# Batch 0's row maxima from float32 scores in four row groups, in a one-core attention and MLP layer

## The reference

```python
q1, q2 = split_heads(x @ Wq1, 16), split_heads(x @ Wq2, 16)      # 16 features a head
k, v = split_heads(x @ Wk, 16), split_heads(x @ Wv, 16)
q = concatenate([q1, q2], axis=1)                                # 32 query heads
scores = einsum('bhqd,bhkd->bhqk', q, repeat(k, 2)) * 0.25       # pairs of query heads share k, v
p = softmax(where(causal, scores, min))
y = p @ repeat(v, 2)
y = y[:, :16] - sigmoid(x @ Wlam) * y[:, 16:]
x = layernorm(x + y @ Wo)
out = layernorm(x + shared_mlp(x) + routed_mlp(x) * comb_w)
```

## Time and profile before

| | |
|---|---|
| median of 3 runs | 467.77 us (466.49 to 467.85) |
| profiled execution, its own time | 466.94 us |
| its span in the profile | 465.2 us |
| busy: PE, VectorE, ScalarE, POOL | 417.3, 282.7, 234.9, 244.6 us |
| granted TensorE clock, mean | 0.958 |
| moved by DMA | 40.41 MB |

### The profile page before, as it was taken

How to read it: one execution, slowest core, us unless ns; L and a number is a source line. 1 busy time by engine, 2 the same in 40 slices (tenths; PEclk the granted TensorE clock), 3 DMA queues, 4 the chain that set the end, 5 groups by cost and what they waited for, 6 DMA issues and landing times.

```text
span 465.2 us, 10336 instructions
## 1 busy us (share of the span) xinstructions
PE 417.3 (90%) x4008; PEld 339.7 (73%) x4008; DVE 282.7 (61%) x676; ACT 234.9 (51%) x532; POOL 244.6 (53%) x334
## 2 busy tenths in 40 slices
PE   4229697899999999999999999999999999997995
PEld 4127246696799768994998669985898579856995
DVE  3637237753658557764758466755767478747474
ACT  4704481539334853567254944476355922592240
POOL 8314483629355754668254945576365922492152
PEclk9859798979999999999999999999999999999899
DMA  8762770346012810363123610381034410000000
GB/s 284 245 162 63 198 196 2 88 117 151 1 46 85 204 46 4 108 156 69 46 61 108 163 46 25 103 198 33 24 85 112 117 46 0 4 1 25 1 25 23
DMA packets 34753, 40.41 MB, mean 87 GB/s; under 512 B 4240, under 2 KB 28304, under 8 KB 34448
## 3 DMA queue, kind: packets, MB, share of 16 engines
q1 hardware_dynamic: 34704, 39.75, 31.6%
HBM read 27.94 MB, written 11.53 MB: 85 GB/s over the span
## 4 chain that ended last, share of the span: by engine, by line
PE 71%; POOL 9%; DVE 8%; ACT 4%; DMA 3%; issue 2%; SPq 2%; POOLq 0%; DVEq 0%; ACTq 0%
PE ff L672 11%; PE ff L673 10%; PE ff L674 10%; PE ring L735 7%; POOL prob L413 6%; PE ybank L787 5%; PE ybank L672 4%; PE ring L730 4%; PE ring L759 3%; PE ybank L673 3%; PE ybank L674 3%; PE ring L763 2%; ACT prob L518 2%; DVE neg_max L1020 2%; PE ybank L800 2%
## 5 line engine op out<-in xcount | busy, mean ns | idle before, releaser
L1020 DVE TENSOR_REDUCE neg_max<-ring 128x2 f32<-128x512 f32 (+3 forms) x176 | 102.7, 638 | 39.1 <-PE ring L735 38.5
L403 POOL TENSOR_TENSOR h_lo<-h_full,h_hi 128x256 fp32r<-128x256 f32 x72 | 52.9, 735 | 101.6 <-ACT h_hi L478 101.6
L413 POOL TENSOR_SCALAR_AFFINE_SELECT prob<-prob 128x512 f32<-128x512 f32 x128 | 82.9, 679 | 15.6 <-ACT prob L518 14.5
L672 PE MATMUL ff<-x1T_hi,wg_lo 128*128 128x256 f32 x288 | 87.2, 303 | 0.0
L518 ACT ACTIVATE prob<-ring 128x512 f32<-128x512 f32 x144 | 78.3, 620 | 6.9 <-PE ring L759 6.9
L673 PE MATMUL ff<-x1T_lo,wg_hi 128*128 128x256 f32 x288 | 81.2, 282 | 0.0
L674 PE MATMUL ff<-x1T_hi,wg_hi 128*128 128x256 f32 x288 | 81.0, 281 | 0.0
L730 PE MATMUL ring<-mask_b,ident_b 128*128 128x128 bf16 (+2 forms) x176 | 45.4, 258 | 18.9 <-DMA q_stack<-qk_parts_dram 17.1
L1041 DVE COPY yv<-ybank 128x256 f32<-128x256 f32 x64 | 27.0, 422 | 56.9 <-PE ybank L787 56.5
L735 PE MATMUL ring<-k_stack,q_stack 96*128 96x256 bf16 (+3 forms) x512 | 60.9, 239 | 0.0
L787 PE MATMUL ybank<-prob,v_ones 128*32 128x256 f32 (+1 forms) x1024 | 56.3, 335 | 2.0 <-POOL prob L413 1.8
(11 more groups left out here) (169 smaller groups left out, 962.7 us busy)
## 6 DMA issues: line engine op xcount, KB each, us to landing
q_stack<-qk_parts_dram SPq DMA_DIRECT2D x48, 256.0 KB, 4.5
qk_parts_dram<-parts SPq DMA_DIRECT2D x72, 128.0 KB
k_stack<-qk_parts_dram SPq DMA_DIRECT2D x48, 128.0 KB, 4.4
xt_raw<-xT SPq DMA_DIRECT2D x8, 256.0 KB, 2.8
xz<-x SPq DMA_DIRECT2D x8, 256.0 KB, 2.8
out<-xz SPq DMA_DIRECT2D x7, 256.0 KB, 2.2
prob<-w_gu SPq DMA_DIRECT2D x1, 1152.0 KB, 7.3
yv<-w_gu SPq DMA_DIRECT2D x1, 1024.0 KB, 9.1
```

Source lines behind the costliest of these rows:

```text
L403: pool.tensor_tensor(h_lo[:, n, :], h_full[:, n % RING, :], h_hi[:, n, :].bitcast(F32), ALU.subtract).then_inc(h_lo_done, 1)
L413: pool.affine_select(out=v, in_=v, compare_op=ALU.is_ge, fill=0.0, base=0, pattern=[[0, 2], [HALF, 2], [0, 2], [1, HALF]], channel_multipl ...
L672: pe.matmul(o, lhs_lo, rhs_hi, start=first, stop=False)
L1020: dve.tensor_reduce(neg_max[:, columns.start:columns.stop, i], ring[u % RING][:, 0:len(columns) * keys].rearrange("p (h k) -> p h k", k=keys),
```

## The change

**First scores.** In batch 0 the 22 units of `s_unit` are replaced by 24 units in six quads (`first_quad`). The queries are copied as float32 from PSUM (`first_query`), and the keys twice (`first_keys`), with a per-partition factor of 1 or 0 so that one copy holds the even heads' keys and one the odd heads' (`make_parity`). The copies lie in the second set of query stacks, unused until batch 1's loads. A head's product then has 32 rows, of which 16 are zero in the keys. The four units of a quad use the four row groups of the array and four banks (`ff` 0 and 1, `ring` 0, `misc`), and their head products are issued in turn. Each unit has a mask matmul as before. A unit of the next quad waits for the maximum of the unit four before. Quad 0 waits for the copies, the first parts and all three rests of batch 0. Behind quad 0 stand the two value jobs, behind quads 1, 2 and 3 the three projection jobs of batch 1. The wait for the stacks stands ahead of the transposed scores.

**Order of the start.** POOL makes the identity matrices first and the memsets of the k_stacks last. SP loads batch 1's x and the first gate/up piece ahead of batch 0's stores, and the other two pieces behind batch 0's twelve loads. Batch 1's parts are stored after `load_max(0)` and after the stacks of batch 0 have landed. ScalarE splits batch 1's x and the first gate/up piece behind batch 0's values, POOL subtracts both (in the kernel before VectorE subtracts all three pieces). The other two pieces are split on ScalarE behind `max_first(0)`, and subtracted on VectorE behind `max_second(0)`, as are w_out and the router.

```diff
+ROW_GROUP = 32
+FIRST_HEADS = HEADS * ROW_GROUP // P
+FIRST_TILE_HEADS = (4, 4, 2, 2)
+FIRST_JOBS = tuple((i, g * FIRST_HEADS + j * heads, heads) for i, heads in enumerate(FIRST_TILE_HEADS)
+                   for j in range(FIRST_HEADS // heads) for g in range(P // ROW_GROUP))
+FIRST_V_AT, FIRST_QK_AT = 0, (1, 2, 3)
...
             def iteration(i, has_next=True, has_last=True):
                 load_x(i)
-                if has_next:
+                if has_next and not is_first(i):
                     store_parts(i + 1, range(QK_JOBS))
                 if i + 2 < B:
                     load_xt(i + 2)
                 load_max(i)
+                if is_first(i):
+                    sp.wait_ge(stack_loaded, 16 * STACK_LOADS)
+                    store_parts(i + 1, range(QK_JOBS))
...
-            for n, (k, cols, raw) in enumerate(GU_PIECES):
-                sp.dma_start(raw, w_gu[k * P:(k + 1) * P, cols]).then_inc(wg_loaded[n], 16)
+            load_xt(1)
+            load_gate_up(0)
             for n, p in ((0, 0), (1, 0), (0, 1), (2, 0), (1, 1), (2, 1), (0, 2), (1, 2), (2, 2)):
                 store_part(0, n, p)
-            load_xt(1)
             load_stacks(0)
+            for n in range(1, len(GU_PIECES)):
+                load_gate_up(n)
...
+            k, cols, raw = GU_PIECES[0]
+            split_xt(1)
+            split_weight(1, wg_lo[:, k, cols], raw, wg_hi[:, k, cols], prob_raw_done)
...
                 split_weight(wp_hi[:, :, proj_chunk(c)], wp_raw[:, :, proj_chunk(c)], wp_loaded[c])
-                if c > 0:
-                    first_part(0, c - 1)
+            first_query(0)
+            first_part(0, 0)
             split_weight(wp_hi[:, :, proj_chunk(QK_JOBS)], wp_raw[:, :, proj_chunk(QK_JOBS)], wp_loaded[QK_JOBS])
-            second_part(0, 0)
+            first_query(1)
+            first_part(0, 1)
+            first_keys()
             first_part(0, QK_JOBS - 1)
-            for n in range(1, QK_JOBS):
+            for n in range(QK_JOBS):
                 second_part(0, n)
             act.wait_ge(consts_made, CONSTS)
             for t in range(TT):
                 values(0, t)
+            split_xt(1)
+            k, cols, raw = GU_PIECES[0]
+            split_weight(wg_hi[:, k, cols], raw, wg_loaded[0], mlp_w_hi_done)
...
+            def first_quad(n):
+                quad = range(QUAD * n, QUAD * (n + 1))
+                if n == 0:
+                    pe.wait_ge(q_first_done, Q_JOBS)
+                    pe.wait_ge(k_first_done, PARITIES)
+                    pe.wait_ge(qk_h_done, QK_JOBS)
+                    pe.wait_ge(qk_rest_done, QK_JOBS)
+                for u in quad:
+                    if n > 0:
+                        pe.wait_ge(max_done, u - QUAD + 1)
+                    i, first, heads = FIRST_JOBS[u]
+                    keys = (i + 1) * HALF
+                    o = first_bank(u)[:, 0:heads * keys].rearrange("p (h k) -> p h k", k=keys)
+                    pe.matmul(o[:, :, keys - HALF:keys], ident_b[:, :], mask_b[:, :].unsqueeze(1).to_broadcast([P, heads, HALF]),
+                              start=True, stop=False, skip_group_check=True)
+                i, _, heads = FIRST_JOBS[QUAD * n]
+                keys = (i + 1) * HALF
+                for j in range(heads):
+                    for u in quad:
+                        row, block = spot(FIRST_JOBS[u][1] + j)
+                        rows = slice(row // 2 * ROW_GROUP, (row // 2 + 1) * ROW_GROUP)
+                        mm = pe.matmul(first_bank(u)[:, j * keys:(j + 1) * keys], q_first[rows, block, i * P:(i + 1) * P],
+                                       k_first[rows, row % PARITIES, block, 0:keys], start=False, stop=True, skip_group_check=True)
+                        if j == heads - 1:
+                            mm.then_inc(s_full, 1)
...
+                for n in range(0 if has_prev else FIRST_QUADS):
+                    first_quad(n)
+                    if n == FIRST_V_AT:
...
+                        for t in range(TT):
+                            v_job(0, t)
+                    if n in FIRST_QK_AT:
+                        qk_job(1, FIRST_QK_AT.index(n))
+                for u in range(S_UNITS if has_prev else 0):
```

More of the change, by code:

```diff
@@ L49 @@
 CONSTS = 6
+PARITIES = 2
 ROUTER_STEPS = 5
@@ L148, in build_layer @@
         minus_half = sb("minus_half", [P, TT])
+        parity = sb("parity", [P, PARITIES])
         gate_t = sb("gate_t", [P, RING, T])
@@ L336, in _ @@
         def _(pool):
+            pool.memset(ident[:, :], 0.0).then_inc(const_step, 1)
+            pool.memset(ident_b[:, :], 0.0).then_inc(const_step, 1)
             pool.memset(xz[2][:, :, :], 0.0).then_inc(consts_made, 1)
             pool.wait_ge(consts_made, 1)
[L339 to L343, removed]
+            pool.wait_ge(const_step, 2)
+            for m in (ident, ident_b):
+                pool.affine_select(out=m[:, :], in_=m[:, :], compare_op=ALU.not_equal, fill=1.0, base=0,
+                                   pattern=[[-1, P]], channel_multiplier=1).then_inc(consts_made, 1)
             pool.memset(mask_b[:, :], 0.0).then_inc(const_step, 1)
@@ L346, in _ @@
             pool.memset(minus_half[:, :], -0.5).then_inc(const_step, 1)
[L347 to L350, removed]
+            pool.wait_ge(const_step, 5)
             for h in range(2):
@@ L358, in _ @@
             pool.memset(v_ones[:, :, :, HEAD_DIM:HEAD_DIM + 1], 1.0).then_inc(consts_made, 1)
+            pool.wait_ge(consts_made, CONSTS)
+            for k_stack in k_stacks:
+                pool.memset(k_stack[STACK_ROWS:STACK_ROWS + MAX_PARTS, :, :, :], 1.0).then_inc(const_step, 1)
+            pool.wait_ge(const_step, 5 + STACKS)
             def split_xt(b):
@@ L427, in iteration @@
             def iteration(i, has_next, has_prev, has_last):
-                if has_next:
+                if has_next and has_prev:
                     split_xt(i + 1)
@@ L482, in split_xt, with first_query, first_keys @@
                 copy(xt_hi[:, :, :], xt_raw[:, :, :]).then_inc(xt_hi_done, 1)
+            def first_query(n):
+                act.wait_ge(qk_full, n + 1)
+                copy(q_first[:, n, :].rearrange("p (i h t) -> p h i t", h=2, i=Q_TILES), psum_order(qk_bank(0, n)[:, :])).then_inc(q_first_done, 1)
+            def first_keys():
+                act.wait_ge(qk_full, QK_JOBS)
+                act.wait_ge(parity_made, PARITIES)
+                for x in range(PARITIES):
+                    act.activation(k_first[:, x, :, :], qk_bank(0, QK_JOBS - 1)[:, :].rearrange("p (n t) -> p n t", n=KEY_BLOCKS), ACT.Copy,
+                                   scale=parity[:, x:x + 1]).then_inc(k_first_done, 1)
             def raw_part(b, n):
@@ L933, in iteration @@
                     gu_units(i - 1, FF_MAX)
+                if not has_prev:
+                    pe.wait_ge(stack_loaded, 16 * STACK_LOADS)
                 pe.wait_ge(max_loaded, (i + 1) * (16 * MAX_PARTS))
@@ L1022, in row_max, with first_max, make_parity @@
                                   negate=True).then_inc(max_done, 1)
+            def first_max(u):
+                dve.wait_ge(s_full, u + 1)
+                i, first, heads = FIRST_JOBS[u]
+                keys = (i + 1) * HALF
+                dve.tensor_reduce(neg_max[:, first:first + heads, i], first_bank(u)[:, 0:heads * keys].rearrange("p (h k) -> p h k", k=keys),
+                                  AX_X, ALU.max,
+                                  negate=True).then_inc(max_done, 1)
+            def make_parity():
+                dve.wait_ge(consts_made, 2)
+                for x in range(PARITIES):
+                    dve.tensor_reduce(parity[:, x:x + 1], ident[:, :].rearrange("p (g x d) -> p x g d", x=PARITIES, d=HEAD_DIM)[:, x, :, :],
+                                      AXES_XY, ALU.add).then_inc(parity_made, 1)
             def max_second(b):
@@ L1167, in iteration @@
                 max_second(i)
+                if not has_prev:
+                    split_weight(W_OUT, wo_lo[:, :, :], wo_raw, wo_hi[:, :, :])
+                    split_weight(W_ROUTER, wr_lo[:, :, :], wr_raw, wr_hi[:, :, :])
+                    for n, (k, cols, raw) in enumerate(GU_PIECES[1:]):
+                        split_mlp_weight(n + 2, wg_lo[:, k, cols], raw, wg_hi[:, k, cols])
+                    dve.wait_ge(v_done, TT)
                 attn[0](dve.tensor_scalar(lam[:, :, :], lam_th[:, :, :], 0.5, 0.5, ALU.mult, ALU.add))
```

93 lines of the change are left out of this document (55 added, 38 removed).

## The result

The changed kernel takes 461.82 us as the median of 4 runs (459.52 to 462.41), the kernel before 467.81 beside it; the ratio is 0.9871, with a 95% interval of 0.9839 to 0.9903. The forecast was 461.0, in a range of 456.5 to 467.0. The profiled execution took 462.41 us, the longest of the four, with a span of 460.7.

A forecast was written before the change was run, and what follows sets the result against it. TensorE bounds the kernel, except early, where batch 0's maxima wait for stack loads until the first transposed score at 52.17. Profiled 466.94 less 6.2 is 460.7; the median was given as 461.0, range 456.5 to 467.0.

The forecast's parts named there:

- The first score: Batch 0's first transposed score matmul, after the maxima land: at 46.0 us against 52.17, 6.2 us less.
- Start of quad 0: First quad of batch 0, right behind VectorE's rest of the keys (job 2): starts at 16.6 us.
- Both of my readings of the row of L787: Float32 column groups, full clock: 49 ns per record or 2.06 ns per column; greater taken per head step, 0.40, 0.53 for 256 keys.
- rival 1: Quads' row groups overlap fully and clock stays up: maxima end at 39.3, scores start at 42.7, 457.5 us; chance 0.25.
- Clock: PE in the quads: quad 0 at 1.2 GHz, and 1.0 us added for quad 4 or 5 at half clock.
- ScalarE ahead of the maxima: Batch 1's split parts before the first maxima: POOL's gate/up piece 5.5 us, ScalarE free at 39.3, 3.6 us before needed, hidden.
- The rule on mode switches: Changing PE's tiling mode drains the engine: twice a quad, twelve times, at 0.2 each 2.4 us more, 463.4.
- the forecast's 0.2 for a handover: Estimated 0.2 us for the handover in each of quads 2 to 5, where PE and VectorE take turns.
- The down weights: End of batch 0: issued 57.6 to 58.8, last landed 65.9; ScalarE's wait hidden before y's split at 68.2, 0.8 us spare.
- the 22.2 that the prediction had named as a sign of being wrong: Batch 0's y split coming later than 22.2 us after the first transposed score would show the prediction wrong.
- Rival 3: Stores and loads take 3 to 4 us longer, so ScalarE is some 3 late for y and value copies: 464.0; chance 0.15.
- the 0.3 us that I added: Final step: 461.0 given, between 460.7 for the profiled execution and a median of runs 0.8 above that execution.

The follow-up runs named there:

- dup_max: Changed kernel with the last eight maxima reductions (quads 4 and 5) each made twice on VectorE; 468.73 us, ratio 1.001 to the kernel before.
- down_early: Changed kernel with the three down-weight loads issued right behind the last two gate/up pieces, ahead of batch 1's stores and stacks; 461.73 us, ratio 0.9871.
- wd_late: Changed kernel with down weights loaded early and ScalarE's three splits of them behind batch 0's y split and batch 1's second values; 461.86 us, ratio 0.9879.
- wd_order: Changed kernel with down weights loaded early, ScalarE's splits behind batch 2's x split, POOL's subtractions behind batch 2's third parts; 457.1 us, ratio 0.9771.
- gu_first: Changed kernel with all three gate/up pieces loaded ahead of batch 0's stores; 461.33 us, ratio 0.9872 to the kernel before.
- second_early: Changed kernel with ScalarE's second part of batch 0's first query job ahead of the first part of the second; 456.8 us, ratio 0.9781.
- by_unit: Changed kernel with a quad's head products issued unit by unit instead of in turn; 468.07 us, ratio 0.9986 to the kernel before.

## Why the prediction was right, and where it was not

- **The first score.** Right: 46.16 against 46.0, 6.0 us earlier against 6.2. dup_max shows that the run follows this point. That it came within 0.2 us is luck: the start 0.7 late and the value jobs with quad 1 1.0 longer are set off by quad 0, 1.0 shorter, and quads 2 to 5, 0.8 shorter. In the four other runs that change only loads or later splits (down_early, wd_late, wd_order, gu_first) it lies between 45.53 and 46.72.
- **Start of quad 0.** 17.34 against 16.6. The second projection job's matmuls came 0.21 us apart up to 11.2 us, not 0.12, though the granted clock of 5.9 to 11.2 reads 1.00, and the key bank was full at 12.8, not 12.0. In the kernel before the pace went to 0.12 at 9.56. That quad 0 waited for VectorE's rest of the keys was right, and second_early shows the price.
- **Head steps.** Both of my readings of the row of L787 were too high; rival 1 was right in kind. 192 keys took 0.32 us and 256 keys 0.43, where I had 0.40 and 0.53, and 64 keys at half clock 0.43, where I had 0.66. That is 1.67 ns per column at full clock when all four groups run. Full overlap did not bring rival 1's time (maxima at 39.3, against 42.56), since its clock did not stay up: 0.54 from 17.3 to 24.7 us, over quad 0, the value jobs and half of quad 1, and 0.55 in quad 5; with that goes the late start.
- **VectorE.** 0.62 and 0.49 as forecast, 0.33 for 256 elements against 0.37. The sum took 2.1 us for each of quads 2 and 3, where its own list has 1.95, which is what they took.
- **Clock.** Half clock in one of the last two quads was right: quad 5, 0.85 us a step.
- **ScalarE ahead of the maxima.** Free at 38.97 against 39.3, POOL's piece 5.10 us against 5.5. Hidden, as said.
- **The rule on mode switches.** Something of this size is there. In quads 2 and 3 the second head record starts 0.43 us after the last mask (27.91 to 28.34, 31.03 to 31.46), where the pace of a mask, 0.06, and of a head record, 0.16, make 0.22: 0.2 us more. In quads 0, 1 and 4 it is 0.1 to 0.3 more, in quad 5 nothing. Switches back to full-array matmuls lie beside VectorE's reductions. Once a quad on the chain this is some 1 us in all, an estimate from these rows; that it is a drain is not shown, and the forecast's 0.2 for a handover, which in fact takes 0.05, made room for it.
- **The down weights.** This step failed: "Hidden, with 0.8 us to spare". The split of y came 23.9 us after the first transposed score, beyond the 22.2 that the prediction had named as a sign of being wrong; the total held because the loss is small against the range. They were issued at 60.4 to 62.5, not 57.6 to 58.8, as I had left out that the loads of batch 1's stacks wait for its stores to land. SP's own waits in the changed kernel:

```profile
SPq L302 <- DMA qk_parts_dram<-parts: 2.3, 1, 2.3
```

  ScalarE stood 6.8 us for them, and the split of y came at 70.10, not 68.2; y itself was there near 67.3. Rival 3 had the late down weights, and priced them at 3.3 us (464.0 against 460.7), nearly twice the 1.9 they cost. The forecast also took the kernel before as free of loss there. It was not: VectorE's two stalls beside POOL cost it 1.7 us, which the change, by moving POOL, gave back.
- **The sum.** 462.41 against 460.7 for the profiled execution: 1.9 us later at the split of y, of which 0.2 was there at the first score. For the median it is 461.82 against 461.0, as the 0.3 us that I added hides a part of it, and as the profiled execution lies 0.6 above the median here, where it lay 0.8 below it in the kernel before. By medians the change is worth 6.0 us, by the profiled executions 4.5.

## What to carry to other kernels

Scores that only serve a row maximum can be made from what PSUM already holds, in small row groups with float32, while the exact operands are on their way. The gain is set by the first point that waits for both, and it is cheap to look next at what that point's neighbours in each queue wait for. Here the order of one ScalarE copy and the place of the down weights' loads and splits were each worth 4 to 5 us by their ratios, where the change is worth 6.0. When one engine's late work is moved, find out which instructions of the other engines it will now lie beside and which it will now stand ahead of.

## What the runs showed of the hardware that was not expected

**PE looks past a few records.** Four float32 records of one row group in a row did not keep the other groups from starting. With eight in a row the next group started beside the fifth (by_unit).

**Executions of one kernel differ by their granted clock.** The four executions of the changed kernel lay between 459.52 us, at a mean clock of 0.972, and 462.41, at 0.960. The same stretch behind batch 1's projections in two profiles, first the changed kernel, then gu_first:

```profile
86.00:93.50 7.50, 7.50 (x42) 6.34 (x42) 5.48 (x12) 1.41 (x4) 1.15 (x1) 0.54 0.36 107
```

```profile
86.00:93.50 7.50, 7.11 (x58) 5.71 (x55) 6.56 (x17) 1.67 (x6) 1.74 (x2) 1.00 0.34 100
```

The one is at 1.2 GHz for nearly all of it, the other at 2.4, and the time from batch 0's add to batch 1's is 49.8 and 47.5 us: 2.3 us for one such stretch, in kernels that differ only in an order of loads 50 us earlier. From 125 to 380 us the clock is 1.00 in all fourteen profiles. Single executions that differ by 2 us can't be put down to an edit here. The landmarks of one profile are not free of this either: quad 0 starts between 16.09 and 17.43 us in the ten kernels without second_early's edit. Distances between landmarks, and medians of several executions, are the safer readings.
